# Moving the turn of x's second tile, S4's sum and two ScalarE steps within a batch's slot of a two-layer LoRA kernel

## Chip, core and metric

The kernel runs on one core of one Trainium2 chip. The time is the device time of one launch in microseconds (us), as the median of several runs.

## What is computed

x has 8 batches of 256 rows with 1024 features, in float32. Two layers are applied, each a "cond" part followed by an "ffn" part, with a residual:

```python
x = x + L0_ffn(L0_cond(x, ids0))     # ffn0: route by the top 1 of 8 logits, LoRA of rank 16, no dense part
x = x + L1_ffn(L1_cond(x, ids1))

def L0_cond(x, ids, W, Wr, A, B):    # dense part + top 2 of 8 experts, softmax over the two, LoRA rank 16
    logits = x @ Wr.T + 5.0 * one_hot(ids)[:, None, :]
    gates = top2_softmax(logits)
    return x @ W.T + 2.0 * einsum('bter,bte,eor->bto', einsum('btd,erd->bter', x, A), gates, B)

def L1_cond(x, ids, W, b, As, Bs):   # dense part + one LoRA pair per batch, picked from 32 by ids
    return x @ W.T + b + 2.0 * (x @ As[ids].T) @ Bs[ids]

def L1_ffn(x, Wb, bb, Wr, A, B):     # dense part + top 2 of 8 experts, softmax, LoRA rank 16
    return x @ Wb.T + bb + 2.0 * einsum(...)(x, top2_softmax(x @ Wr.T), A, B)
```

## The kernel before

**Setup (to about 178 us).** The weights of the layers are folded into each other, so that each tile of x needs few products: C0 gives layer 0's gate logits and low-rank inputs, M (the product of layer 1's two dense weights, with the identity added for the residual) gives layer 1's output. Each float32 operand is kept as two parts, hi and lo, and each product is three matmuls (`three`, lines 1403 to 1405: hi by hi, hi by lo, lo by hi). M's columns past the first 256 are cut into seven right factors for a Strassen-like scheme.

**Slots (from about 178 us to the end).** A loop goes over the eight batches b. One slot holds layer 1 of batch b (tiles m = 2b and m+1) and, between its matmuls, layer 0 of the next batch (tiles a = 2b+2 and a+1). `has_a` says that there is a next batch, `has_n` that there is one after it, whose x (tiles n = 2b+4 and n+1) is loaded in this slot. The order of the work is written out by hand, engine by engine, and semaphores with fixed counts join the engines. All engines take their instructions in that order.

- TensorE (`slot`, from line 1560 on): small0(a) is the product of x with C0. main_to(n) advances the long list of 44 steps (16 of the direct columns, then seven products A11, S2, A22, S1, A12, S3, S4 of four steps each). Between them stand short products and transposes: turn_small of hg, wh, wz (line 1455), add_lora0 (the product with D0, needs hgTlo), adapter, lora, and ffn0 in four quarters.
- VectorE: gates0 makes hg out of small0's result. The low parts of the turned tiles (hgT_part, whT_part, wzT_part, line 927), the gates of layer 1 (gates1), the top 1 (top1, makes wh), the sums S1 to S4 of blocks of x (s_sums, lines 1109 to 1117), the sums of layer 0's output with x (x1_add, line 1090), the kept products (keep_p16, keep_p15, keep_p167) and the output's sums (y_c21, y_c22, y_c12; all line 1121) follow in a row. turn_x (line 978) turns a tile of x in 32x32 blocks, in place.
- ScalarE copies the high parts (line 667): xT_turned(t, half) of a turned tile of x, into xThi; s_part of a sum; hgT_part, whT_part, wzT_part of a turned small tile; exp0 and exp1 are the exponentials of the gates; keep_p1 (line 751) copies product A11 out of its bank; y_direct copies the direct columns.
- GpSimd makes the low parts of xT and of S3 and S4 (line 607).
- SyncE issues the loads and stores in order. Of one slot: the load of as (lora_As), x's half 0 of the batch after next, Ebuf, x's half 1, Fbuf, the stores.

x_raw has two buffers, one for each parity of b. The load of half 0 writes the buffer out of which slot b's sums are made. SP waits for the last of the sums, by its count:

```python
if more_x:
    sp.wait_ge(s_raw, b * 4 + 4)
    load_x(b * 2 + 4, 0, x_raw[turn])     # four transfers of 128 KB
if not last:
    sp.wait_ge(z1_done, m + 2)
    load_e(b + 1)
if more_x:
    sp.wait_ge(s34_lo, b * 2 + 2)
    load_x(b * 2 + 5, 1, x_raw[turn])
```

s_sums adds one to s_raw for each of its four sums; the last one, nth = 3 (line 1117), is S4's: A12 - A22, which reads the half that the load overwrites.

Of the kernel before, what the change touches and what calls it, by code (L numbers as in the profile page):

```python
# [23 lines left out]
def adaln_ffn(nc, x, lang_ids, slot_ids, W0, Wr0, A0c, B0, route_w, A0f, Bw, W1, b1, lora_As, lora_Bs,  # L24
              Wb, b_base, W_router, A1, B1, out):
    NB, SEQ, D = x.shape
# [29 lines left out]
    with ctx:  # L56
# [97 lines left out]
        x_raw = [x_raw0, x_raw1]  # L154
# [42 lines left out]
        x_in = [sem(f"x_in{i}") for i in range(2)]  # L197
# [458 lines left out]
        def _(act):  # L656
# [42 lines left out]
            def xT_turned(t, half, raw):  # L699
                if not isinstance(t, int) or t > 2:  # L700
                    act.wait_ge(p0_done, t)
                for h in range(2):
                    hi_half(x_turned, t - 1, half_of(xT[0], h), raw_block(raw, half, h), xT_hi)
# [11 lines left out]
            def exp1(t):  # L715
                act.wait_ge(max1_ready, t + 1)
                act.activation(G1["ex"][:, :], G1["mx"][:, 0:1], ACT.Exp, bias=G1["mx"][:, 1:2], scale=-1.0)\
                   .then_inc(exp1_ready, 1)

            def hgT_part(t):  # L720
                wait_earlier(act, z0_done, t)
                hi_half(thg_done, t + 1, hgThi[:, :], pt_hg, hgT_hi)
# [11 lines left out]
            def s_part(q, turn, nth):  # L734
                name = ("S1", "S2", "S3", "S4")[nth]
                if nth < 2:

                    wait_earlier(act, p_done, q * 7 - 1 + nth if not isinstance(q, int) or q > 0 else 0)
                elif nth == 2:
                    act.wait_ge(h1_done, q * 2 + 2)  # L740
                else:
                    act.wait_ge(p_done, q * 7 + 1)
                j = (1, 1, 0, 1)[nth]
                hi_half(s_raw, q * 4 + (1, 3, 2, 4)[nth], left_of(turn)[name][:, 0, :], raw_block(x_raw[turn], 1, j), s_hi)

            def keep_p1(b):

                act.wait_ge(p_done, b * 7 + 1)
                wait_earlier(act, y_out[0], b * 16)
                y0, n = Y_OF[1]  # L750
                act.activation(ybuf[0][:, y0:y0 + n], ca, ACT.Copy).then_inc(p1_kept, 1)
# [122 lines left out]
            def slot(b, turn, has_a, has_n):  # L874
                m, a, n, q = b * 2, b * 2 + 2, b * 2 + 4, b + 1
                if not isinstance(b, int) or b > 0:
                    s_part(b, turn, 1)
                if has_a:
                    exp0(a)
                if isinstance(b, int) and b == 0:  # L880
                    s_part(b, turn, 1)
                if has_a:
                    xT_turned(a + 1, 1, x_raw[1 - turn])
                    hgT_part(a)
                s_part(b, turn, 2)
                hsT_part(m, 0)
                hsT_part(m + 1, 1)
                if has_a:
                    whT_part(a, 0)
                exp1(m)  # L890
                keep_p1(b)
                s_part(b, turn, 3)
                exp1(m + 1)
                wzT_part(m)
                if has_a:
                    exp0(a + 1)
                    hgT_part(a + 1)
                if has_n:
                    xT_turned(n, 0, x_raw[turn])
                y_direct(b, 0)  # L900
                wzT_part(m + 1)
                if has_a:
                    whT_part(a + 1, 1)
                    as_part(b + 1)
                    a_part(q, 1 - turn, 0)
                    a_part(q, 1 - turn, 1)
                y_c11(b)
                if has_a:
                    a_part(q, 1 - turn, 2)
                    a_part(q, 1 - turn, 3)  # L910
                y_direct(b, 1)
                if has_a:
                    s_part(q, 1 - turn, 0)
# [10 lines left out]
        def _(dve):  # L924
# [50 lines left out]
            def turn_x(half, raw):  # L975

                tile = raw[:, half * D:(half + 1) * D]
                dve.transpose(tile, tile).then_inc(x_turned, 1)  # L978
# [18 lines left out]
            def gates0(t, b, meanwhile=None):  # L997
                dve.wait_ge(p0_done, t + 1)
                dve.tensor_tensor(G0["lg"][:, :], p0[:, ER:ER + E], bias[:, bass.ds(b * E, E)], ALU.add).then_inc(lg0_ready, 1)
                iota_there()  # L1000
                dve.wait_ge(lg0_ready, t + 1)
                gates_from(G0, G0["lg"][:, :], t, g0_step, max0_ready, exp0_ready, meanwhile)
                wait_earlier(dve, thg_done, t)
                spread(hg[:, :], p0[:, 0:ER], G0["g"]).then_inc(hg_ready, 1)
# [93 lines left out]
            def s_part(q, turn, nth):  # L1098
                left = left_of(turn)[("S1", "S2")[nth]]
                dve.wait_ge(s_hi, q * 4 + nth + 1)  # L1100
                lo(left[:, 1, :], raw_block(x_raw[turn], 1, 1), left[:, 0, :]).then_inc(s12_lo, 1)
# [25 lines left out]
            def keep_p16(b):  # L1127
                dve.wait_ge(p_done, b * 7 + 2)
                dve.wait_ge(p1_kept, b + 1)
                wait_earlier(dve, y_out[0], b * 16)  # L1130
                add_y(0, 2, cb, p1_of(), c_kept)
# [188 lines left out]
            def slot(b, turn, has_a, has_n):  # L1320
                m, a, n, q = b * 2, b * 2 + 2, b * 2 + 4, b + 1
                raw = x_raw[1 - turn]

                if has_a:
                    gates0(a, q, first_sums if b == 0 else None)
                s_part(b, turn, 1)
                hs_part(m, 0)
                if has_a:
                    hgT_part(a)
                s_sums(b, turn, (3,))  # L1330
                hs_part(m + 1, 1)
                if has_a:
                    top1(a)
                if b == 0:
                    lo_last((T2, T4))
                gates1(m, 0, (lambda: whT_part(a, 0)) if has_a else None)
                gates1(m + 1, 1, None)
                wzT_part(m)
                if b == 0:
                    lo_last((T1,))  # L1340
                if has_a:
                    gates0(a + 1, q)
                if b == 0:
                    lo_last((T3,))
                keep_p16(b)
                if has_a:
                    hgT_part(a + 1)
                keep_p15(b)
                if has_n:
                    dve.wait_ge(x_in[0], b * 64 + 64)  # L1350
                    turn_x(0, x_raw[turn])
                if has_a:
                    top1(a + 1)
                wzT_part(m + 1)
                if has_a:
                    whT_part(a + 1, 1)
                    as_part(q)
                if has_a:
                    x1_add(q, 0, raw)
                    x1_add(q, 1, raw)  # L1360
                    x1_add(q, 2, raw)
                    a_part(q, 1 - turn, 0)
                keep_p167(b)
                if has_a:
                    x1_add(q, 3, raw)
                    a_part(q, 1 - turn, 1)
                    a_part(q, 1 - turn, 2)
                    a_part(q, 1 - turn, 3)
                if has_a:
                    s_sums(q, 1 - turn, (0, 1))  # L1370
                y_c21(b)
                y_c22(b)
                if has_a:
                    s_part(q, 1 - turn, 0)
                    s_sums(q, 1 - turn, (2,))
                y_c12(b)
                if has_n:
                    dve.wait_ge(x_in[1], b * 64 + 64)
                    turn_x(1, x_raw[turn])
            slot(0, 0, True, True)  # L1380
            for b in range(1, NB - 3):
                slot(b, b % 2, True, True)
# [6 lines left out]
        def _(pe):  # L1389
# [35 lines left out]
            def turn_x(src, at):  # L1425
                for h in range(2):
                    for k in range(4):
                        ins = pe.transpose(rows(at[h], k), rows(src, 4 * h + k), ident[:, :])
                    ins.then_inc(tx_done, 1)
# [148 lines left out]
            def slot(b, turn, has_a, has_n, first=False):  # L1578
                m, a, n, q = b * 2, b * 2 + 2, b * 2 + 4, b + 1
# [131 lines left out]
                if has_a:  # L1711
                    pe.wait_ge(whT_lo, a + 2)
                    pe.wait_ge(y_act, b * 3 + 1)
                    for g in range(4):
                        if g:
                            pe.wait_ge(x1_sum, q * 4 + g)
                        ffn0(q, g, x1w)
                        main_to((42, 43, 43, 44)[g] if first else (39, 40, 42, 43)[g])
                        if g < 2:
                            lora(m + 1, 1, g)  # L1720
                if not has_a:
# [39 lines left out]
```

## Time and profile before

| | us |
|---|---|
| median of 3 runs | 484.27 (483.86 to 485.82) |
| profiled execution | 484.3 |
| its span | 482.1 |
| TensorE busy | 465.5 (97%) |
| VectorE busy | 327.2 (68%) |
| ScalarE busy | 154.5 (32%) |
| GpSimd busy | 75.5 (16%) |

The span goes from the first to the last instruction of the profile; the execution's own time is 2.2 us longer. Busy shares are means over the whole span. A matmul's duration reaches over the start of the next ones, so the distance between two starts is what one costs. In timelines, the bracket at the end of a row is the idle time of the engine before the row, and what ended it. The granted clock is that of TensorE, as a share of full speed.

### The profile page before, as it was taken

The page shows a single profiled execution, that of the slowest core. Times are in us where ns is not written, and L with a number is a line of the kernel's source. Part 1 is how long each engine was busy: PE and PEld are TensorE (multiplying, and loading weights), DVE is VectorE, ACT ScalarE, POOL GpSimd, SP SyncE. Part 2 cuts the span into 40 slices and gives each one's busy share as a digit, 9 for nine tenths or more (in the row PEclk, how much of TensorE's full clock was granted, in tenths as well). Part 3 has the DMA queues.
Part 4 walks back from the last instruction along what each step waited for, and adds up shares of the span by engine and source line. Part 5 has one row for each costly group of instructions (what it writes and reads, how often), then busy time and mean ns, then how long its engine had stood idle before and what let it go on. Part 6 is the DMA issues. An engine that isn't in the chain of part 4 may idle for free.

```text
span 482.1 us, 8344 instructions
## 1 busy us (share of the span) xinstructions
PE 465.5 (97%) x2911; PEld 430.1 (89%) x2911; DVE 327.2 (68%) x956; ACT 154.5 (32%) x340; POOL 75.5 (16%) x64
## 2 busy tenths in 40 slices
PE   6998999999999999999999999999999999999996
PEld 5987998999999789888999999999999999999985
DVE  3857755584776598849649848857865965963842
ACT  4565430232312364224223313323423323421320
POOL 2021000000000332221220240240221222130110
PEclk9999999999999999999999999999999999999999
DMA  8994548211112101223223321520520432300202
GB/s 268 384 286 163 143 142 148 105 44 45 44 45 52 42 16 28 31 44 111 46 46 107 50 46 61 95 44 16 133 43 7 122 46 33 110 2 2 103 2 87
DMA packets 88545, 40.25 MB, mean 83 GB/s; under 512 B 68503, under 2 KB 82465, under 8 KB 88382
## 3 DMA queue, kind: packets, MB, share of 16 engines
q1 hardware_dynamic: 88414, 39.81, 31.6%
q0 software_dynamic: 96, 0.00, 0.3%
q8 instruction: 19, 0.31, 0.3%
q14 instruction: 16, 0.13, 0.1%
HBM read 28.64 MB, written 11.16 MB: 83 GB/s over the span
## 4 chain that ended last, share of the span: by engine, by line
PE 77%; DVE 17%; issue 2%; ACT 2%; DMA 2%; SPq 0%; DVEq 0%; ACTq 0%
PE banks L1403 22%; PE banks L1405 22%; PE banks L1404 22%; PE banks L1419 4%; PE banks L1398 3%; DVE left L927 3%; DVE ybuf L1121 2%; DVE x_raw L978 2%; PE banks L1652 1%; PE banks L1455 1%; DVE b_acc L1218 1%; DVE G L927 1%; DMA fe_lo_dram<-fe_keep_lo 1%; DVE x_raw L1090 1%; ACT left L667 1%
## 5 line engine op out<-in xcount | busy, mean ns | idle before, releaser
L1403 PE MATMUL banks<-G,left 128*128 128x460 f32 x224 | 88.0, 393 | 0.0
L1404 PE MATMUL banks<-G,left 128*128 128x460 f32 x224 | 82.9, 370 | 0.0
L1405 PE MATMUL banks<-G,left 128*128 128x460 f32 x224 | 82.9, 370 | 0.0
L607 POOL TENSOR_TENSOR xTlo<-x_raw,xThi 128x512 fp32r<-128x512 f32 x28 | 41.1, 1486 | 252.3 <-ACT xThi L667 114.8
L1403 PE MATMUL banks<-WbThi,ws_hi 128*128 128x460 f32 (+1 forms) x216 | 75.2, 348 | 0.5 <-DVE Mdir L927 0.5
L1405 PE MATMUL banks<-WbThi,ws_lo 128*128 128x460 f32 (+1 forms) x216 | 73.4, 340 | 0.0
L1404 PE MATMUL banks<-WbTlo,ws_hi 128*128 128x460 f32 (+1 forms) x216 | 73.0, 338 | 0.0
L667 ACT ACTIVATE left<-x_raw 128x512 fp32r<-128x512 f32 x64 | 38.8, 628 | 64.1 <-DVE x_raw L1090 29.3
L1403 PEld LDWEIGHTS banks<-G,left 128*128 128x128 f32 x224 | 42.3, 189 | 4.5 <-DVE wzTlo L927 0.3
L1405 PEld LDWEIGHTS banks<-G,left 128*128 128x128 f32 x224 | 42.1, 188 | 4.6
L1404 PEld LDWEIGHTS banks<-G,left 128*128 128x128 f32 x224 | 42.3, 189 | 2.6
L1403 PEld LDWEIGHTS banks<-WbThi,ws_hi 128*128 128x128 f32 x216 | 40.6, 188 | 3.7 <-DVE ws_lo L927 0.6
L1404 PEld LDWEIGHTS banks<-WbTlo,ws_hi 128*128 128x128 f32 x216 | 40.8, 189 | 3.3
L1405 PEld LDWEIGHTS banks<-WbThi,ws_lo 128*128 128x128 f32 x216 | 40.6, 188 | 3.0
L1121 DVE TENSOR_TENSOR ybuf<-banks,ybuf 128x460 f32<-128x460 f32 x48 | 29.7, 631 | 12.5 <-PE banks L1405 11.7
L1090 DVE TENSOR_TENSOR x_raw<-banks,x_raw 128x512 f32<-128x512 f32 x28 | 19.4, 692 | 26.0 <-PE banks L1405 25.1
L1403 PE MATMUL banks<-Mdir,left 128*128 128x256 f32 x128 | 36.5, 285 | 0.2 <-DVE left L927 0.2
L1404 PE MATMUL banks<-Mdir,left 128*128 128x256 f32 x128 | 35.9, 281 | 0.0
L1405 PE MATMUL banks<-Mdir,left 128*128 128x256 f32 x128 | 35.9, 280 | 0.0
L607 POOL TENSOR_TENSOR left<-x_raw,left 128x512 fp32r<-128x512 f32 x16 | 20.7, 1312 | 85.7 <-DVE hg L994 61.1
L927 DVE SCALAR_TENSOR_TENSOR left<-x_raw,left 128x512 fp32r<-128x512 f32 x48 | 32.2, 684 | 1.1 <-ACT left L667 0.7
L1403 PE MATMUL banks<-C0hi,xThi 128*128 128x272 f32 x112 | 32.3, 288 | 0.3 <-DVE ws_lo L927 0.3
(213 smaller groups left out, 1004.6 us busy)
## 6 DMA issues: line engine op xcount, KB each, us to landing
x_raw<-in_x_dram SPq DMA_DIRECT2D x56, 128.0 KB, 3.6
out_dram<-ybuf SPq DMA_DIRECT2D x14, 512.0 KB, 2.8
x_raw<-in_L_cond_W_dram SPq DMA_DIRECT2D x10, 512.0 KB, 6.7
wraw<-in_L_cond_W_dram SPq DMA_DIRECT2D x5, 512.0 KB, 5.6
wraw<-in_L_ffn_W_base_dram SPq DMA_DIRECT2D x4, 512.0 KB, 10.2
x_raw<-in_L_ffn_W_base_dram SPq DMA_DIRECT2D x4, 512.0 KB, 9.3
a0f<-in_L_ffn_A_dram SPq DMA_DIRECT2D x2, 512.0 KB, 9.7
xin_first<-in_x_dram SPq DMA_DIRECT2D x1, 1024.0 KB, 15.3
```

What stands on the lines that cost most here:

```text
L607: return gp.tensor_tensor(out_, a, b, ALU.subtract)
L667: act.activation(dst, src, ACT.Copy).then_inc(ready, 1)
L927: return dve.scalar_tensor_tensor(out=out_, in0=src, scalar=scale, in1=hi.bitcast(F32), op0=ALU.mult, op1=ALU.subtract)
L978: dve.transpose(tile, tile).then_inc(x_turned, 1)
L1090: dve.tensor_tensor(raw_quarter(raw, g), by_half(x1w), raw_quarter(raw, g), ALU.add).then_inc(x1_sum, 1)
L1121: return dve.tensor_tensor(ybuf[tile][:, y0:y0 + n], bank, base, ALU.add).then_inc(ready, 1)
L1218: dve.scalar_tensor_tensor(out=b_acc[:, c0:c0 + w], in0=Wb_of[c][n][:, k, :].bitcast(F32), scalar=bcol[:, k:k + 1], in1=b_acc[:, c0:c0 + w ...
L1398: ins = pe.transpose(unit_bank(q)[:, col:col + width], src, ident[0:kp, 0:kp])
L1403: pe.matmul(out_, l[0], r[0], start=start, stop=False, **kw)
L1404: pe.matmul(out_, l[0], r[1], start=False, stop=False, **kw)
L1405: return pe.matmul(out_, l[1], r[0], start=False, stop=stop, **kw)
L1419: ins = pe.matmul(banks[:, k, 0:2 * RC], w, R0T[:, j, :], start=j == 0 and n == 0, stop=j == K - 1 and n == 1)
```

## The change

On VectorE the turn of the second tile of x (half 1) leaves the end of slot b for the place behind gates0 in slot b+1, so it is done in slots 1 to 6; S4's sum leaves the place between hgT_part(a) and the second hs_part for that behind keep_p16. On ScalarE hgT_part(a) and xT_turned change places, keep_p1 goes behind the second exp1, and the copy of S4's high part goes behind hgT_part(a + 1). On TensorE, in the first slot, the third quarter of ffn0 is followed by two steps of the list, where it was one. SP and GpSimd keep their order.

```diff
@@ ScalarE, slot
                 if has_a:
+                    hgT_part(a)
                     xT_turned(a + 1, 1, x_raw[1 - turn])
-                    hgT_part(a)
                 s_part(b, turn, 2)
                 hsT_part(m, 0)
                 hsT_part(m + 1, 1)
                 if has_a:
                     whT_part(a, 0)
                 exp1(m)
+                exp1(m + 1)
                 keep_p1(b)
-                s_part(b, turn, 3)
-                exp1(m + 1)
                 wzT_part(m)
                 if has_a:
                     exp0(a + 1)
                     hgT_part(a + 1)
+                s_part(b, turn, 3)
                 if has_n:
                     xT_turned(n, 0, x_raw[turn])
@@ VectorE, slot
                 if has_a:
                     gates0(a, q, first_sums if b == 0 else None)
+                if 0 < b < NB - 1:
+
+                    dve.wait_ge(x_in[1], b * 64)
+                    turn_x(1, x_raw[1 - turn])
                 s_part(b, turn, 1)
                 hs_part(m, 0)
                 if has_a:
                     hgT_part(a)
-                s_sums(b, turn, (3,))
                 hs_part(m + 1, 1)
@@
                 keep_p16(b)
+                s_sums(b, turn, (3,))
                 if has_a:
                     hgT_part(a + 1)
                 keep_p15(b)
@@
                 y_c12(b)
-                if has_n:
-                    dve.wait_ge(x_in[1], b * 64 + 64)
-                    turn_x(1, x_raw[turn])
@@ TensorE, slot
-                        main_to((42, 43, 43, 44)[g] if first else (39, 40, 42, 43)[g])
+                        main_to((42, 43, 44, 44)[g] if first else (39, 40, 42, 43)[g])
```

## Rows read from the trace of the kernel before

**Rows 1.** Page, busy time of each engine: us, share of the span, instructions.

```profile
PE 465.5 (97%) x2911; PEld 430.1 (89%) x2911; DVE 327.2 (68%) x956; ACT 154.5 (32%) x340; POOL 75.5 (16%) x64
```

**Rows 2.** Who waited for whom on TensorE from 178 us: us, times, longest.

```profile
PE banks L1455 <- DVE hg L994: 3.2, 6, 1.1
```

**Rows 3.** Timeline of VectorE over a slot's edge: start, us, line, tiles.

```profile
299.90 0.63 DVE L1121 TENSOR_TENSOR ybuf<-banks,ybuf 128x460 f32<-128x460 f32 x1
300.44 1.24 DVE L978 STREAM_TRANSPOSE x_raw<-x_raw 128x1024 f32<-128x1024 f32 x1
301.60 0.13 DVE L999 TENSOR_TENSOR lgc<-banks,bias 128x8 f32<-128x8 f32 x1
...
303.63 0.29 DVE L994 TENSOR_TENSOR hg<-banks,gc 128x128 f32<-128x128 f32 x1
...
304.74 0.28 DVE L927 SCALAR_TENSOR_TENSOR hgTlo<-banks,hgThi 128x128 fp32r<-128x128 f32 x1
304.94 1.28 DVE L1117 TENSOR_TENSOR x_raw<-x_raw 128x512 f32<-128x512 f32 x1
```

**Rows 4.** Timeline of TensorE at the same edge.

```profile
303.97 0.33 PE L1455 MATMUL banks<-ident,hg 128*128 128x128 f32 x1 [0.41 <-DVE hg L994]
...
305.48 0.23 PE L1403 MATMUL banks<-D0hi,hgThi 128*128 128x136 f32 x1
```

**Rows 5.** Timeline of VectorE in the slot's middle.

```profile
315.58 0.29 DVE L994 TENSOR_TENSOR hg<-banks,gc 128x128 f32<-128x128 f32 x1
315.79 0.63 DVE L1121 TENSOR_TENSOR ybuf<-banks,ybuf 128x460 f32<-128x460 f32 x1
318.13 0.29 DVE L927 SCALAR_TENSOR_TENSOR hgTlo<-banks,hgThi 128x128 fp32r<-128x128 f32 x1 [1.71 <-ACT hgThi L667]
...
319.57 1.24 DVE L978 STREAM_TRANSPOSE x_raw<-x_raw 128x1024 f32<-128x1024 f32 x1
...
323.20 0.29 DVE L927 SCALAR_TENSOR_TENSOR wzTlo<-banks,wzThi 128x128 fp32r<-128x128 f32 x1 [0.87 <-ACT wzThi L667]
```

**Rows 6.** SP's loads of x (one slot, fourth issue, all landings); S4's sum.

```profile
306.42 3.32 SPq L405 DMA_DIRECT2D x_raw<-in_x_dram  x4
...
L405 SPq DMA_DIRECT2D x_raw<-in_x_dram x1: 912/912/912, 308.8 to 308.8; - x1
...
DMA to landing us min/median/max: 3.0/3.6/4.1
...
L1117 DVE TENSOR_TENSOR x_raw<-x_raw x8: 682/1281/1285, 188.5 to 455.9; 128x512 f32<-128x512 f32 x8
```

**Rows 7.** Timeline of ScalarE in the slot's middle.

```profile
320.90 1.15 ACT L667 ACTIVATE xThi<-x_raw 128x512 fp32r<-128x512 f32 x2 [2.81 <-DVE x_raw L978]
321.96 0.24 ACT L757 ACTIVATE ybuf<-banks 128x104 f32<-128x104 f32 x1
322.89 0.28 ACT L667 ACTIVATE wzThi<-banks 128x128 fp32r<-128x128 f32 x1 [0.69 <-PE banks L1455]
```

**Rows 8.** Timeline of TensorE in the slot's middle.

```profile
323.88 0.27 PE L1455 MATMUL banks<-ident,wh 128*128 128x128 f32 x1
```

**Rows 9.** Slot 0, timelines of VectorE and of TensorE's weight loads.

```profile
201.47 0.63 DVE L1121 TENSOR_TENSOR ybuf<-banks,ybuf 128x460 f32<-128x460 f32 x1
...
206.75 0.28 DVE L927 SCALAR_TENSOR_TENSOR wzTlo<-banks,wzThi 128x128 fp32r<-128x128 f32 x1
...
207.08 0.19 PEld L1403 LDWEIGHTS banks<-G,left 128*128 128x128 f32 x1 [0.32 <-DVE wzTlo L927]
```

**Rows 10.** Stretches: length, busy us (instructions), granted clock, DMA share, GB/s.

```profile
479.00:481.00 2.00, 0.00 (x0) 0.00 (x0) 0.00 (x0) 0.00 (x0) 0.00 (x0) 1.00 0.46 173
481.00:482.10 1.10, 0.00 (x0) 0.00 (x0) 0.00 (x0) 0.00 (x0) 0.00 (x0) 0.52 0.00 0
...
8.00:13.00 5.00, 5.00 (x23) 5.00 (x24) 1.00 0.89 354
14.00:17.00 3.00, 3.00 (x26) 3.00 (x25) 1.00 1.07 365
```

## The prediction

> **What bounds the kernel now.** I read the chain of waits first, then the waits of TensorE, then the timelines of one repeated slot. The page gives TensorE 97% of the span [rows 1]. From 178 us on, where the eight slots run, TensorE's only repeated wait is for hg, the first tile that the gates produce in a slot: 3.2 us over six slots, 1.1 in the longest [rows 2]. So nearly nothing can be won and much can be lost, and a change of order has to be priced by what TensorE will wait for next. I work on the slot that begins at 300 us. Slots 1 to 5 repeat it with a period of about 38.5 us; slot 0, with the last right factors still being made, is taken by itself.
>
> VectorE runs without a gap over the slot's edge: y_c12 at 299.90, the turn of the second tile at 300.44, the gates from 301.60, hg at 303.63, hgTlo at 304.74, S4's sum at 304.94 [rows 3]. TensorE waits 0.41 us and turns hg at 303.97; its next product from this chain (D0, line 1403) starts at 305.48 [rows 4].
>
> **Part 1, the turn of the second tile moves behind gates0 (slots 1 to 6).** The turn takes 301.60-300.44 = 1.16 us of VectorE. Without it in front, hg is ready at 303.63-1.16+0.29 = 302.76, before TensorE wants it, so the wait goes. But the turn now stands between hg and hgTlo, so hgTlo stays at 304.74. A stalled TensorE starts 0.34 us after the start of the VectorE operation that it waits for (303.63 to 303.97). So D0 can start at 304.74+0.34 = 305.08, where it started at 305.48: the next wait in line leaves 0.40 of the stall's 0.4 to 0.6 us. Putting hgT_part ahead of xT_turned on ScalarE is what allows it: xT_turned would wait for the later turn. Ends for this part: 0 (hgTlo later by the contention of some other write) and 0.6 (the whole stall) a slot; I take 0.4. It holds in slots 1 to 6. xTlo on GpSimd starts some 0.7 us later than before, but loses its contention with S4's sum, and small0 follows 4 us behind; 0.
>
> **Part 2, S4's sum moves behind keep_p16.** Its 1.2 us leaves a place where the engine then waits for TensorE's turn of hs anyway, and enters one where VectorE idles 1.71 us before hgTlo [rows 5]. On VectorE alone it costs nothing. What hangs on it is SP's queue: slot_dmas waits for s_raw = 4b+4, which is this sum, before it issues the load of the next x (x_raw, half 0) into the buffer that the sum reads. That load's issue is not moved in the code, but it moves with the sum. And VectorE, right after keep_p15, waits for the same load to turn it.
>
> - Now: the sum starts at 304.94, SP issues the four 128 KB transfers from 306.42, 1.48 us later, the fourth at 308.8; issue to landing is 3.0 to 4.1 us, median 3.6 [rows 3, 6]. The turn starts at 319.57, 7 us after the landing: the load is hidden.
> - Changed (with the slot 0.40 earlier by part 1): hg at 315.58-0.40 = 315.18, keep_p16 0.21 later at 315.39, the sum 0.54 behind it at 315.93 [rows 3, 5]. GpSimd makes S3's low part then, so I keep the sum's contended 1.28 us; alone it takes 0.68 [rows 6]. SP issues at 315.93+1.48 = 317.41. The fourth issue is 2.4 later and, taking 3.7 us for it, lands at 323.5. The turn starts at 323.55, against 319.57.
> - Behind the turn, in order: on ScalarE xThi (+1.33), the y copy (another +1.06), then wzThi, which I put 0.14 behind the start of that 0.24 us copy, since ends overlap: turn+2.53; VectorE's wzTlo follows wzThi by 0.31, at turn+2.84 [rows 5, 7]. VectorE's own way over top1 needs turn+2.68 and is shorter. TensorE must have wzTlo before it may turn wh. So it turns wh at 323.55+2.84+0.34 = 326.73, where it did at 323.88 [rows 8]: **+2.85 us a slot**, part 1's 0.40 already in it.
>
> After that, wh to whTlo to ffn0 and the x1 sums follow TensorE as before, so nothing of the loss is given back. The rest of SP's queue (Ebuf's three loads, then x's half 1) slides behind the late load to about 325; its users stand a slot's edge away.
>
> Slot 0: keep_p16 at 201.47, so the sum at 202.01, issue 203.49, landing 209.6, turn 209.65, wzTlo 212.49, TensorE 212.83, where it now starts at 207.08 behind a wait of 0.32 for wzTlo [rows 9]: **+5.75**. Here TensorE has three steps more ahead of the wait, but VectorE's chain stands some 4 us nearer to it.
>
> The range of the load: from first issue to last landing 2.4+3.0 = 5.4 to 2.4+4.1 = 6.5, I take 6.1; over six slots -4.2 to +2.4 us. The sum uncontended would save 0.6 a slot, 3.6 in all.
>
> The Trainium skill (DMA: Bandwidth & Descriptors, Rules for kernel authors) tells to issue a DMA early and wait on its semaphore late, so that its fixed cost overlaps with compute; this change issues late and leaves the wait where it is. The trace of before shows the early form, with 7 us to spare.
>
> **Part 3, the small ones.** keep_p1 behind the second exp1 is ready near 312; its readers are keep_p16 at 315.8 and a product at about 319: 0. S4's high part on ScalarE goes behind hgT_part(a+1), about 318, and S4's low part on GpSimd ends near 320; the S4 product comes near 329: 0. If that cover were gone it would be a wait of the same load chain, not a new one. In slot 0 TensorE takes step 43 ahead of the last quarter of ffn0, into a 0.8 us wait for x1; but that slot's end is set by VectorE's row of work behind the same x1 sum, so 0 (at best 0.6).
>
> **Part 4, TensorE's clock.** The change makes TensorE stand still for about 3 us five times and 5.7 us once. In the trace the granted clock is 1.00 in 479 to 481 us, with no matmul, and 0.52 in 481 to 482.1 [rows 10]: it falls (2.4 to 1.2 GHz) after 2 to 3 us of standing still. At the start of the kernel, behind a wait of 4.3 us, 23 matmuls of 272 columns take 5 us, and later 26 take 3 us [rows 10]: dense work at about half rate for 5 us (there the granted column says 1.00; I go by the spacing). Time at half rate costs half of itself: 0 to 2.7 us for a stall; I take the middle, 1.4. Waits of up to 1.3 us never lowered it. For slot 0 I take the fall as given, for the others at three of five: 4 x 1.4 = **+5.6**.
>
> The Trainium skill (TensorE: Matmul & The Clock Gate, HAM oscillation) describes this pattern: matmul bursts between DMA waits of some us re-throttle the clock every time. By it all six would fall: 6 x 1.4 = 8.4 instead of 5.6.
>
> **Sum.** 5.75 + 5 x 2.85 - 0.40 (slot 6, which loads nothing) = +19.6; with the clock +25.2. On the profiled execution's own 484.3 us (span 482.1 and 2.2 around it) 509.5; the median of the runs, 484.27, is the same number.
>
> **Rivals.**
> - The clock holds in all stalls: 484.3+19.6 = 503.9. For it: a stall of 3 us is barely as long as what lowered the clock at the end. Against: slot 0's is twice that. 25%.
> - It falls in all six: 484.3+19.6+8.4 = 512 at 1.4 us each, 520 if it stays low as long as at the start (6 x 2.7). For it: the same rows. Against: there the first matmuls were sparse turns of small tiles, here work is dense at once. 12%.
> - The load lands sooner (5.4) and the sum runs alone (0.68): 1.3 less a slot, -7.8: 496 with a full clock, 502 with 5.6 for it. For it: the minimum landing 3.0. Against: the fourth transfer lands late, and GpSimd is at work then. 10%.
> - On the other side: the load does not hang on S4's sum, since the count on which SP waits is met by another sum, and the turn finds its tile. It decides from a first issue before about 313. Then part 1 alone is left: 6 x 0.40, 481.9. Against: each slot makes four counts, 4b+4 is its last, and the same sum reads the half that the load overwrites. 4%.
> - Something behind the late load is late as well (half 1, Ebuf): 3 us more a slot, 525. Nothing in the timelines speaks for it. 4%.
>
> **How the numbers follow.** The forecast has 45%, with 505 to 514 for its own range; the rivals 25, 12, 10, 4 and 4. From 501 to 517 holds the forecast, the first rival and part of the two beside it, about 8 in 10. No change within 0.5% (about what a measurement of this kernel can tell) has 1%, faster 4%, slower 95%.
>
> **What would show it.** In the profile after: SP's issue of x_raw half 0 about 11 us later in each slot; VectorE idle for some 4 us ahead of the turn, released by a DMA; TensorE waiting about 3 us (slot 0: 5.7) for wzTlo, six times; no wait for hg, instead a short one for hgTlo at D0; granted clock under 1.00 in slices behind the stalls. Wrong would be: no DMA as releaser on VectorE, or a stall under 2 us a slot.

## The result, and the profile after

The changed kernel takes 517.02 us (513.06 to 519.46, 4 runs) beside 484.2: a ratio of 1.0674, 95% interval 1.0636 to 1.0712. The forecast was 509.5 in a range of 501 to 517, so the time lies at the range's edge, and beyond the 505 to 514 that I had given the forecast without its rivals. The profiled execution took 519.1 us, with a span of 516.9; the one before 484.3 and 482.1.

The page of the changed kernel: span, busy times, and the granted clock in 40 slices (in tenths; against one row of nines before).

```profile
span 516.9 us, 8348 instructions
...
PE 480.8 (93%) x2911; PEld 440.4 (85%) x2911; DVE 332.7 (64%) x956; ACT 154.1 (30%) x340; POOL 70.3 (14%) x64
...
PEclk9999999999999999799989989989997997999999
```

TensorE's work is the same (x2911), and its busy time is up by 15.3 us, at a mean granted clock of 0.967 over the span. Below, its waits for wzTlo from 178 us on (us in total, times, longest); line 1456 is line 1455 of before. The wait for hg [rows 2] is no longer among the large ones.

```profile
PE banks L1456 <- DVE wzTlo L927: 17.1, 5, 3.9
PE banks L1404 <- DVE wzTlo L927: 5.1, 1, 5.1
```

The same view of VectorE names the transfer as the releaser, in each of the six slots that load:

```profile
DVE x_raw L978 <- DMA x_raw<-in_x_dram: 28.5, 6, 5.4
```

One slot of the changed kernel, in the order of the chain. First VectorE's timeline (start, us, line, tiles, idle before), which answers to [rows 5]:

```profile
333.89 0.29 DVE L994 TENSOR_TENSOR hg<-banks,gc 128x128 f32<-128x128 f32 x1
334.10 0.63 DVE L1121 TENSOR_TENSOR ybuf<-banks,ybuf 128x460 f32<-128x460 f32 x1
334.64 1.55 DVE L1117 TENSOR_TENSOR x_raw<-x_raw 128x512 f32<-128x512 f32 x1
336.26 0.29 DVE L927 SCALAR_TENSOR_TENSOR hgTlo<-banks,hgThi 128x128 fp32r<-128x128 f32 x1
337.15 0.64 DVE L1121 TENSOR_TENSOR ybuf<-banks,ybuf 128x460 f32<-128x460 f32 x1 [0.60 <-PE banks L1406]
342.41 1.25 DVE L978 STREAM_TRANSPOSE x_raw<-x_raw 128x1024 f32<-128x1024 f32 x1 [4.62 <-DMA x_raw<-in_x_dram]
...
345.24 0.29 DVE L927 SCALAR_TENSOR_TENSOR wzTlo<-banks,wzThi 128x128 fp32r<-128x128 f32 x1
```

S4's sum now stands at 334.64, 0.75 us behind hg. SP issues the load of x behind it (SP's timeline; [rows 6] had it 13 us before the turn):

```profile
336.39 2.99 SPq L405 DMA_DIRECT2D x_raw<-in_x_dram  x4
```

VectorE's turn at 342.41 waits 4.62 us for it. From the turn the way leads over ScalarE (its timeline, as [rows 7]), back to wzTlo at 345.24, and to TensorE's turn of wh, which waits 3.41 us [rows 8]:

```profile
343.75 1.15 ACT L667 ACTIVATE xThi<-x_raw 128x512 fp32r<-128x512 f32 x2 [6.89 <-DVE x_raw L978]
344.80 0.24 ACT L757 ACTIVATE ybuf<-banks 128x104 f32<-128x104 f32 x1
344.94 0.27 ACT L667 ACTIVATE wzThi<-banks 128x128 fp32r<-128x128 f32 x1
```

```profile
345.58 0.48 PE L1456 MATMUL banks<-ident,wh 128*128 128x128 f32 x1 [3.41 <-DVE wzTlo L927]
```

Then the clock. Two stretches of the same slot (length, busy us and instructions of PE, PEld, DVE, ACT and POOL, granted clock, DMA share, GB/s): the stall, and the 5.4 us of dense work behind it.

```profile
341.90:345.50 3.60, 0.28 (x2) 0.00 (x0) 2.72 (x9) 1.46 (x4) 0.16 (x1) 0.82 0.76 119
345.60:351.00 5.40, 5.40 (x19) 4.94 (x19) 2.22 (x3) 0.50 (x2) 2.25 (x2) 0.50 0.09 14
```

The first is at full clock for most of the stall, the second at 0.50, the 1.2 GHz level, with 19 matmuls in 5.4 us. Half rate for 5.4 us of full work is 2.7 us lost by this estimate, nearly as much as the stall itself.

The clock does not have to fall inside the stall. The same view for slot 1, whose stall goes from 254.62 to 258.54: it is at full clock throughout, and half clock begins 0.3 us after TensorE has started again.

```profile
254.70:258.50 3.80, 0.00 (x0) 0.00 (x0) 2.75 (x9) 1.46 (x4) 0.20 (x1) 1.00 0.60 90
258.90:262.20 3.30, 3.30 (x13) 2.98 (x13) 0.52 (x2) 0.50 (x2) 2.03 (x2) 0.50 0.27 40
```

TensorE's turns of hg and wh (its transposes of these tiles) mark the same places in both kernels, so their distances give a ledger (us, changed minus before; worked out from the timelines of TensorE):

| slot | lag added by the stall | from the stall to wh of the next slot |
|---|---|---|
| 0 | 5.5 (and 1.1 at half rate up to wh) | 1.0 |
| 1 | 4.1 | 1.3 |
| 2 | 3.8 | 1.3 |
| 3 | 3.6 | 2.2 |
| 4 | 3.3 | 2.4 |
| 5 | 3.2 | 2.5 |
| sum | 23.3 + 1.1 | 10.8 |

Together 35.2, with 0.4 won back at the kernel's end: the span's 34.8. The right column is the clock less what the moved turn wins at the slot's edge. All of this is one execution. The other three runs had granted clocks of 0.967, 0.977 and 0.983, and the last of them was at half clock for about half as long (510.9 x 0.017 x 2 = 17 us, against 34 us here); how many of its stalls lowered the clock is not on record. What the moved turn leaves is the wait for hgTlo, on TensorE's weight loads:

```profile
PEld banks L1404 <- DVE hgTlo L927: 3.2, 6, 0.9
```

### The profile page after: what moved, and what is told of

The parts are those of the page before. It is cut to its first block, busy times and chain, and to the rows that moved or that the text cites. A ratio compares the mean times of both kernels' runs of the same rounds, so it can differ in the third digit from the quotient of the medians.

```text
span 516.9 us, 8348 instructions
## 1 busy us (share of the span) xinstructions
PE 480.8 (93%) x2911; PEld 440.4 (85%) x2911; DVE 332.7 (64%) x956; ACT 154.1 (30%) x340; POOL 70.3 (14%) x64
## 4 chain that ended last, share of the span: by engine, by line
PE 60%; DVE 23%; DMA 7%; issue 4%; ACT 3%; SPq 3%; DVEq 0%; ACTq 0%
PE banks L1404 18%; PE banks L1406 17%; PE banks L1405 17%; DMA x_raw<-in_x_dram 5%; PE banks L1420 3%; DVE x_raw L978 3%; SPq L405 2%; PE banks L1399 2%; DVE ybuf L1121 2%; DVE left L927 2%; DVE x_raw L1117 2%; DVE G L927 2%; DMA wraw<-in_L_cond_W_dram 1%; DVE b_acc L1218 1%; PE banks L1653 1%
## 5 line engine op out<-in xcount | busy, mean ns | idle before, releaser
L1404 PE MATMUL banks<-G,left 128*128 128x460 f32 x224 | 91.6, 409 | 5.1 <-DVE wzTlo L927 5.1
L1406 PE MATMUL banks<-G,left 128*128 128x460 f32 x224 | 86.5, 386 | 0.0
L1405 PE MATMUL banks<-G,left 128*128 128x460 f32 x224 | 86.5, 386 | 0.0
L607 POOL TENSOR_TENSOR xTlo<-x_raw,xThi 128x512 fp32r<-128x512 f32 x28 | 35.5, 1290 | 286.0 <-ACT xThi L667 243.3
L1404 PEld LDWEIGHTS banks<-G,left 128*128 128x128 f32 x224 | 44.5, 199 | 9.7 <-DVE wzTlo L927 5.5
L1406 PEld LDWEIGHTS banks<-G,left 128*128 128x128 f32 x224 | 44.5, 199 | 5.1
L1405 PEld LDWEIGHTS banks<-G,left 128*128 128x128 f32 x224 | 44.5, 199 | 2.8
L978 DVE STREAM_TRANSPOSE x_raw<-x_raw 128x1024 f32<-128x1024 f32 x14 | 17.2, 1236 | 28.5 <-DMA x_raw<-in_x_dram 28.5
L927 DVE SCALAR_TENSOR_TENSOR left<-x_raw,left 128x512 fp32r<-128x512 f32 x48 | 32.0, 680 | 1.1 <-ACT left L667 0.7
```

What stands on the lines that cost most here:

```text
L607: return gp.tensor_tensor(out_, a, b, ALU.subtract)
L927: return dve.scalar_tensor_tensor(out=out_, in0=src, scalar=scale, in1=hi.bitcast(F32), op0=ALU.mult, op1=ALU.subtract)
L1404: pe.matmul(out_, l[0], r[0], start=start, stop=False, **kw)
L1405: pe.matmul(out_, l[0], r[1], start=False, stop=False, **kw)
L1406: return pe.matmul(out_, l[1], r[0], start=False, stop=stop, **kw)
```

## The experiments

**S4's sum put back.**

```diff
                     hgT_part(a)
+                s_sums(b, turn, (3,))
                 hs_part(m + 1, 1)
@@
                 keep_p16(b)
-                s_sums(b, turn, (3,))
```

> The changed kernel with S4's sum put back between hgT_part(a) and the second hs_part; the moved turn, ScalarE's order and TensorE's first slot stay as changed. Theory (the loss hangs on the place of S4's sum, because SP's load of x waits for it): all stalls for wzTlo are gone, the clock stays full, and only the gain of the moved turn is left, 0.3 to 0.4 us in six slots: 482.2 us, 481.5 to 483. Rival (the moved turn or ScalarE's new order costs part of the loss): well above 485, and 500 if it is half of it.

Measured: 483.23 us (10 runs), ratio to before 0.9983 (0.9968 to 0.9998). The whole loss hangs on this one line. The gain that is left is 1 us, not 2, and the time is 0.2 over the range that I had given. TensorE's weight loads in it wait for two things of VectorE:

```profile
PEld banks L1404 <- DVE hgTlo L927: 3.2, 6, 0.9
...
PEld banks L1456 <- DVE wh L994: 0.5, 3, 0.2
```

and the sum, which now runs into GpSimd's later xTlo, takes 1.65 us where it took 1.28 [rows 3]:

```profile
304.70 1.65 DVE L1117 TENSOR_TENSOR x_raw<-x_raw 128x512 f32<-128x512 f32 x1
```

**S4's sum alone.** The kernel before, with

```diff
                 keep_p16(b)
+                s_sums(b, turn, (3,))          # VectorE; taken from behind hgT_part(a)
@@
                     hgT_part(a + 1)
+                s_part(b, turn, 3)             # ScalarE; taken from behind keep_p1
```

> The kernel before with one thing changed: S4's sum behind keep_p16, with ScalarE's copy of it behind hgT_part(a+1) (without that the two engines would wait for each other). Theory: the whole loss and no gain, the changed kernel's 517 plus some 2: 519 us, 514 to 523, with six waits for wzTlo and granted clock 0.5 behind them. Rival (the loss needs the turn's move as well): under 500.

Measured: 516.57 us (5 runs), 1.0668 (1.0634 to 1.0701). That is the changed kernel's time with only the sum and ScalarE's copy of it moved. The moved turn's gain can't be seen beside it, since the changed kernel's own runs spread over 6.4 us. TensorE's waits (total, times, longest) are the changed kernel's for wzTlo, and beside them those for hg of before:

```profile
PE banks L1455 <- DVE wzTlo L927: 17.9, 5, 4.1
PE banks L1403 <- DVE wzTlo L927: 5.1, 1, 5.1
PE banks L1455 <- DVE hg L994: 3.1, 6, 1.1
```

Together with the first run this is both directions: without the line no loss, with it alone all of it.

**The sum late, but the wait for the load late as well.** The changed kernel with

```diff
-                if has_n:                      # VectorE, ahead of top1(a + 1)
-                    dve.wait_ge(x_in[0], b * 64 + 64)
-                    turn_x(0, x_raw[turn])
@@
                     x1_add(q, 1, raw)
+                    if has_n:
+                        dve.wait_ge(x_in[0], b * 64 + 64)
+                        turn_x(0, x_raw[turn])
@@
-                if has_n:                      # ScalarE, ahead of y_direct(b, 0)
-                    xT_turned(n, 0, x_raw[turn])
@@
                     a_part(q, 1 - turn, 1)
+                if has_n:
+                    xT_turned(n, 0, x_raw[turn])
                 y_c11(b)
```

> The changed kernel, S4's sum late as in it, but VectorE's wait for the load and the turn of the first tile stand behind the second x1_add, some 9 us later in the slot, and ScalarE's xT_turned(n, 0) ahead of y_c11. Theory (the loss is a wait for a transfer issued late, nothing else of the late sum): 482.3 us, 481.5 to 484, no wait for wzTlo of over 0.5 us, SP's load as late as in the changed kernel. Rival (the late load or the sum beside GpSimd harms by contention, or the turn only moves the wait to small0 of the next slot): 490 or more.

Measured: 487.5 us (5 runs), 1.0069 (1.0042 to 1.0096), granted clock 1.00. 29.5 of the 33 us are back with the transfer issued as late as before, so the late issue by itself is not the price, the wait is. The last 5 us over my 482.3 are a miss of the theory (4 us over the 483.2 of the first run): the turn has moved, and with it GpSimd's low part of xT, into the stretch where VectorE has few gaps. VectorE's and GpSimd's timelines there:

```profile
331.22 1.24 DVE L978 STREAM_TRANSPOSE x_raw<-x_raw 128x1024 f32<-128x1024 f32 x1
...
333.39 1.71 DVE L927 SCALAR_TENSOR_TENSOR left<-x_raw,left 128x512 fp32r<-128x512 f32 x1
```

```profile
333.26 2.99 POOL L607 TENSOR_TENSOR xTlo<-x_raw,xThi 128x512 fp32r<-128x512 f32 x2 [10.52 <-ACT xThi L667]
```

The low part of A11 at 333.39 takes 1.71 us beside GpSimd, where the same operation takes 0.68 alone (it is L927 on left; 0.65 to 0.68 in the undisturbed places of this trace). Of the 2.2 us that this row gains in a slot (1.16 for the turn, 1.03 for the longer low part), TensorE sees a part: hg and what follows it come late in every slot, as its waits show. How the 4 to 5 us divide between the two was not tested.

```profile
PEld banks L1404 <- DVE hgTlo L927: 5.7, 6, 1.0
PEld banks L1404 <- DVE ybuf L1121: 2.3, 3, 1.5
PEld banks L1456 <- DVE hg L994: 2.0, 7, 0.3
```

**TensorE kept at work in the stall.** The changed kernel with

```diff
                 main_to(37 if first else 36)
+                if has_n:
+                    for _ in range(42 if first else 24):
+                        pe.matmul(zd[1][:, :], BwThi[:, 0:P], BwThi[:, P:P + DW], start=False, stop=False, ...)
                 pe.wait_ge(wzT_lo, m + 2)
```

> The changed kernel with matmuls of 256 columns without use ahead of TensorE's wait for wzTlo, 24 in a slot (2.8 us) and 42 in slot 0 (4.9 us), so that TensorE doesn't stand still there; they add to the second tile's direct columns, whose output is therefore not the reference's. Theory (10 to 13 us of the 33 lost are the clock that falls in the stalls): granted clock 1.00, the waits stay as long by VectorE's clock, 506 us, 504 to 508.5. Rival (the waits cost all of it and the clock is a side show): 515 or more.

Measured: 505.03 us (4 runs, 504.72 to 505.19), 1.0427 (1.0394 to 1.046). One slot on TensorE: the 24 added matmuls fill 3.02 us, 0.52 are left as a wait. The granted clock on its page is 9 (90% or more) in every slice.

```profile
335.11 3.02 PE L1709 MATMUL banks<-BwThi 128*128 128x256 f32 x24
338.65 0.33 PE L1456 MATMUL banks<-ident,wh 128*128 128x128 f32 x1 [0.52 <-DVE wzTlo L927]
```

```profile
PEclk9999999999999999999999999999999999999999
```

So 517.0-505.0 = 12.0 us of the loss are the clock, and 505.0-484.2 = 20.8 the stalls less the moved turn's gain. Between the two profiled spans it is 13.9 us; by the ledger above, the stalls of this execution add up to 22.9 and not 23.3, which leaves about 13.4 for the clock. That its runs lie within 0.5 us, and the changed kernel's within 6.4, suggests that the spread comes from the clock too: in its four runs the granted clock was 0.967, 0.967, 0.977 and 0.983 at spans of 516.9, 517.3, 512.8 and 510.9.

**Half of that.** The same, with 12 matmuls (26 in slot 0).

```diff
-                    for _ in range(42 if first else 24):
+                    for _ in range(26 if first else 12):
```

> The changed kernel with 12 matmuls without use ahead of the wait for wzTlo (26 in slot 0) in place of 24 (42), which leave TensorE standing still for some 2 us in each stall; they add to the second tile's direct columns, whose output is not the reference's. If the clock falls only behind stalls of nearly 3 us: granted clock 1.00 and 505 us, as with 24. If 2 us are enough: falls in most slots and 512 to 517. In between, with falls in some slots: 506 to 512.

Measured: 508.92 us (4 runs, 505.8 to 510.82), 1.0493 (1.0465 to 1.0521). TensorE stood still for 1.7 to 2.4 us in each of the six slots. Its waits in slots 1 to 5:

```profile
PE banks L1456 <- DVE wzTlo L927: 9.9, 5, 2.4
```

In its profile the clock fell behind three of the six stalls. A stretch at half clock (behind the stall that ends at 341.65), and one that kept full clock (over the stall from 297.94 to 299.63 and behind it):

```profile
342.00:345.50 3.50, 3.50 (x13) 3.21 (x13) 0.53 (x3) 0.50 (x2) 2.04 (x2) 0.51 0.11 12
298.00:305.00 7.00, 5.37 (x33) 5.08 (x34) 3.20 (x11) 2.27 (x7) 2.64 (x2) 1.00 0.35 56
```

It fell behind stalls of 2.36, 2.13 and 1.96 us and held behind those of 2.17, 1.77 and 1.68 us, so the length alone does not sort them. In the changed kernel's profile, stalls of 3.0 to 5.1 us lowered it six times out of six.

**The turn alone.** The kernel before with turn_x(1) behind gates0 and hgT_part(a) ahead of xT_turned, and nothing else.

```diff
                     gates0(a, q, first_sums if b == 0 else None)
+                if 0 < b < NB - 1:
+                    dve.wait_ge(x_in[1], b * 64)
+                    turn_x(1, x_raw[1 - turn])     # taken from the end of the slot
@@
+                    hgT_part(a)
                     xT_turned(a + 1, 1, x_raw[1 - turn])
-                    hgT_part(a)
```

> The kernel before with the turn of x's second tile behind gates0 and hgT_part(a) ahead of xT_turned, and nothing else. Theory (keep_p1's place, the place of S4's copy on ScalarE and TensorE's list in slot 0 are worth nothing): the same as the changed kernel with the sum put back, 483.3 us, 482.8 to 483.9. Rival (one of the small edits carries the gain or a loss): different from it by more than 1 us.

Measured: 483.99 us (12 runs), 1.0001 (0.9986 to 1.0017). It is within 1 us of the run with the sum put back, as expected, and 0.1 over the range that I had given; the intervals of the two overlap. In the profiled executions the way from slot 0's first turn of hg to the last turn of wz (both on TensorE) takes 281.8 us here, 281.7 with the sum put back and 282.2 before: over the slots the small edits show nothing, and the moved turn some 0.4 us in all. Between the medians the small edits could be worth up to 0.8 us.

**hgTlo sooner.** The changed kernel, sum put back, and

```diff
-                s_part(b, turn, 1)
                 hs_part(m, 0)
                 if has_a:
                     hgT_part(a)
+                s_part(b, turn, 1)
```

> The changed kernel with S4's sum put back, and the low part of S2 behind hgT_part(a). It takes away the wait for hgTlo (0.4 us a slot) and leaves that for wh, since VectorE's work up to wh is the same. Theory (wh ends last there): no better than with the sum put back, 483.2 us, 482.6 to 483.7. Rival (hgTlo's wait was the price): 0.3 us less in six slots, 481.4.

Measured: 484.32 us (12 runs), 1.0003 (0.9992 to 1.0014): no better, in fact 0.6 over my range, and not for my reason. The wait for hgTlo is gone, and TensorE's weight loads wait for the second hs instead, which follows S2's low part and the contended sum (1.66 to 1.67 us here). wh was not the next in line:

```profile
PEld banks L1658 <- DVE hs L927: 3.8, 6, 0.9
```

**The sum in another gap.** The last kernel, with the sum between top1(a) and gates1(m).

```diff
                 s_part(b, turn, 1)
-                s_sums(b, turn, (3,))
                 hs_part(m + 1, 1)
                 if has_a:
                     top1(a)
+                s_sums(b, turn, (3,))
```

> The changed kernel with S4's sum between top1(a) and the first gates1, and the low part of S2 behind hgT_part(a), so that hgTlo comes 0.6 us sooner. Theory (the load of x has 7 us to spare and is hidden wherever it is issued before some 313 in a slot that begins at 300; behind the wait for hg the waits for hgTlo and for wh take back all but 0.1 us a slot of the moved turn's gain, and both go here): no wait for hg, hgTlo, wh or wzTlo in slots 1 to 6, 0.6 us less in six slots, 480.6 us, 480 to 482. Rival (the 0.7 us that VectorE does before gates1 shows in a later wait, for wz or the second hg): 483 to 485. Rival (the load late again): over 490.

Measured: 481.7 us (5 runs, 480.66 to 482.16), 0.9954 (0.9941 to 0.9967), faster than both kernels, by 0.5% for the one before. VectorE's and SP's timelines of one slot:

```profile
306.39 0.68 DVE L1117 TENSOR_TENSOR x_raw<-x_raw 128x512 f32<-128x512 f32 x1
...
317.56 1.24 DVE L978 STREAM_TRANSPOSE x_raw<-x_raw 128x1024 f32<-128x1024 f32 x1
```

```profile
307.27 3.52 SPq L405 DMA_DIRECT2D x_raw<-in_x_dram  x4
```

GpSimd's low part of xT is done by then, and the sum takes 0.68 us. The load is issued at 307.27, and the turn at 317.56 does not wait for it. The waits for hg, hgTlo and hs are gone from the repeated slots; one of a quarter of a us for wh is left. The time is 2.5 us below before's, and not the 3.6 that I expected. The profiled span, at 478.5, is 3.6 below, but 0.8 of that comes before slot 0's first turn of hg; from there to the last turn of wz it is 279.7 us for 282.2, so the slots win 2.5, or 0.4 each in six.

```profile
PEld banks L1456 <- DVE wh L994: 1.6, 6, 0.5
```

## Why the prediction was right, and where its sizes were off

The mechanism, the stalls and the direction came as forecast. The time still came 7.5 us over the forecast, and that is one term, the clock: with its measured 12 us in place of 5.6 the sum would be 515.9. That 517.0 is no further off than the edge of 501 to 517 is owed to a range made wide for the rivals.

- **The load issued behind the sum, and VectorE waiting for it: right.** All the marks came: SP's issue late, VectorE released by a DMA, six waits for wzTlo. The two runs around the single line show it from both sides, and the run with the turn late shows that it is the wait and not the late issue.
- **The stalls: 22.0 us forecast (5.75, and five times 2.85 with the 0.40 of part 1 put back), 23.3 measured.** In slot 0 the stall was 5.5 for 5.75. In the slot shown the steps were: issue 1.75 us behind the sum's start (forecast 1.48, the sum took 1.55 and not 1.28), issue to turn 6.02 (6.14), turn to wzTlo 2.83 (2.84), wzTlo to TensorE 0.34 (0.34). In slots 1 and 2 SP took 4.1 us over the four issues and not 3, and the turn came 6.5 us behind the issue in slot 1. These two slots were 0.8 and 0.5 over the forecast, the other four between 0.3 over and 0.3 under it: 1.3 us in all.
- **The moved turn: 0.40 us a slot forecast, about 0.25 measured** (0.22 to 0.30 in the run with added matmuls, where the clock stays full: hg's turn comes 0.5 sooner in slots 2 to 6, and some 0.27 is given back up to wh). With the sum in its old place 0.1 to 0.2 is left. The sum then meets GpSimd's later xTlo, and in my expectation for that run I had priced that pair at nothing.
- **The clock is the term that was mis-sized: 5.6 us forecast, 12 to 13.4 measured.** In the profiled execution it fell for all six stalls and not for four; and it cost 2.0 to 2.2 us each on average and not 1.4, as work ran at half rate for 3.4 to 6.1 us behind a stall. (The 2.7 that I gave as the upper end for one stall is more than the half of the 5 us in [rows 10].) The rival "it falls in all six" named 512 at 1.4 each and 520 at 2.7. The measured 517 lies between the two; I gave that rival 12%, and it was the one that happened. The row at the kernel's end had pointed to it: the clock was lowered after 2 to 3 us without a matmul [rows 10], and all the forecast stalls were as long.
- The rule that I had set beside it, of the Trainium skill (TensorE: Matmul & The Clock Gate, HAM oscillation), that bursts of matmuls between DMA waits re-throttle the clock each time, agrees with this trace: six of six, for stalls of 3.0 to 5.1 us. The 8.4 worked out by it was nearer than my 5.6, and still short of 12.
- **The small edits at nothing:** right to within 1 us by the medians, and nothing over the slots of the profiled executions.

## What to carry to other kernels

Before moving an instruction, look up which counts it adds to and who waits for them: here a sum of 0.7 to 1.5 us was moved into a gap that fitted it, and a transfer queue two engines away moved with it, into a wait of 4 to 5 us. When a change makes the bounding TensorE stand still for 2 us or more, price the clock with it: here it added more than half of the stall again (12 beside 21 us) for stalls of 3 to 5 us, and fell behind three of six stalls of 1.7 to 2.4 us. And when a gap has been found for an operation, look at who shares its neighbourhood: the place that won was the one where the sum met neither the load nor GpSimd.

## What the runs showed of the hardware that I had not expected

- Behind stalls of 3.0 to 5.1 us, the clock was back only 3.7 to 6.1 us after TensorE had started again, with 3.4 to 6.1 us of work at half rate; in slots 1 and 2 it fell only when TensorE was already at work (0.3 and 1.1 us behind the stall's end). Stalls of 1.96, 2.13 and 2.36 us lowered it and one of 2.17 did not. In the kernel before, waits of up to 1.3 us never did so.
- A VectorE operation with both inputs in SBUF (the sum: x_raw twice; the low part: x_raw and left) grows when GpSimd is at work on its own: the sum takes 0.68 us alone and 1.28, 1.55 and 1.65 beside GpSimd, the low part 0.68 alone and 1.71. In these four pairs, in the slots shown, VectorE's operation started 0.73, 1.00, 1.10 and 1.16 us before the end of the GpSimd operation that was running, and took 0.60, 0.87, 0.97 and 1.03 us longer than alone: the excess is what was left of GpSimd's operation, less 0.13. The Trainium skill (SBUF — State Buffer, Who interferes with whom) says that a VectorE instruction with two inputs in SBUF contends with a GpSimd instruction that reads SBUF, and that the pair of ports they share is an exclusive lock; these numbers agree with it. One such pair's measured time therefore does not carry over to another place: it depends on who starts first and by how much.
